# A buffer for every output block, late stores on ScalarE's queue, and two sums with x ahead of the statistics

## What is computed

```python
xn = layernorm(x)
qkv = einsum('bld,ed->ble', xn, w_qkv)          # q and k get the rotation
attn = softmax(einsum('blhd,bmhd->bhlm', q, k) * scale)
a = einsum('bld,ed->ble', einsum('bhlm,bmhd->blhd', attn, v), w_out)
f = einsum('bsh,dh->bsd', silu(xn @ wg.T) * (xn @ wu.T), wd)   # wg, wu, wd = integers / 127
out = x + a + f
```

## Time and profile before

| | us |
|---|---|
| median of 3 runs | 2934.07 (2931.21 to 2934.49) |
| the profiled execution | 2935.97 |
| its span | 2934.2 |
| PE busy | 2854.9 (97%) |
| DVE busy | 2667.8 (91%) |
| ACT busy | 2480.9 (85%) |
| POOL busy | 636.2 (22%) |

### The profile page before, as it was taken

How to read it: one execution, slowest core, us unless ns; L and a number is a source line. 1 busy time by engine, 2 the same in 40 slices (tenths; PEclk the granted TensorE clock), 3 DMA queues, 4 the chain that set the end, 5 groups by cost and what they waited for, 6 DMA issues and landing times.

```text
span 2934.2 us, 67972 instructions
## 1 busy us (share of the span) xinstructions
PE 2854.9 (97%) x27582; PEld 1052.0 (36%) x27582; DVE 2667.8 (91%) x2946; ACT 2480.9 (85%) x4639; POOL 636.2 (22%) x1214
## 2 busy tenths in 40 slices
PE   6999999999999999999999999999999999999997
PEld 4666664333333333333333333333333333333334
DVE  7667666999999999999999999999999999999952
ACT  4544555999999999999999999999999999999972
POOL 4666673011111111111111111111111111111110
PEclk9999997999999999999999999999999999999999
DMA  3233331111111111111111111111111111111125
GB/s 116 86 96 116 100 95 55 25 31 31 31 31 31 31 31 31 31 31 31 31 31 32 31 31 31 32 31 31 31 31 31 31 31 31 31 31 31 31 66 177
DMA packets 128700, 137.18 MB, mean 47 GB/s; under 512 B 43264, under 2 KB 111488, under 8 KB 128384
## 3 DMA queue, kind: packets, MB, share of 16 engines
q1 hardware_dynamic: 128384, 132.79, 16.7%
HBM read 88.15 MB, written 34.08 MB: 42 GB/s over the span
## 4 chain that ended last, share of the span: by engine, by line
PE 86%; ACT 5%; DVE 4%; issue 2%; DMA 1%; POOL 0%; SPq 0%; POOLq 0%; DVEq 0%; ACTq 0%
PE psum L764 37%; PE psum L729 21%; PE psum L800 17%; PE psum L635 5%; PE psum L606 4%; ACT probs L966 3%; ACT acc_sb L936 1%; DVE row_max L1390 1%; PE psum L650 1%; ACT hT L860 1%; DVE stats L1139 1%; PE psum L710 0%; DVE xnT L1163 0%; DVE h L1305 0%; DMA out_y<-y_in 0%
## 5 line engine op out<-in xcount | busy, mean ns | idle before, releaser
L1390 DVE TENSOR_REDUCE row_max<-psum 128x1 f32<-128x1024 f32 x2018 | 2297.2, 1217 | 23.8 <-PE psum L729 23.8
L966 ACT ACTIVATE probs<-psum 128x512 f32<-128x512 f32 x4096 | 2179.2, 595 | 159.2 <-PE psum L800 52.9
L764 PE MATMUL psum<-probs,v_op 128*32 128x256 f32 x15872 | 1297.6, 399 | 0.0
L800 PE MATMUL psum<-q_op,k_op 51*128 51x512 f16 x4096 | 854.4, 381 | 20.7 <-ACT probs L966 15.6
L729 PE MATMUL psum<-k_op,q_op 48*128 48x512 f16 x4066 | 808.0, 389 | 5.2 <-DVE row_max L1390 2.7
L729 PEld LDWEIGHTS psum<-k_op,q_op 48*128 48x128 f16 x4066 | 196.7, 93 | 853.1 <-DVE row_max L1390 543.5
L764 PEld LDWEIGHTS psum<-probs,v_op 128*32 128x32 f32 x15872 | 312.5, 108 | 525.2 <-issue 493.4
L800 PEld LDWEIGHTS psum<-q_op,k_op 51*128 51x128 f16 x4096 | 365.2, 94 | 252.3 <-ACT probs L966 70.9
L1118 POOL TENSOR_TENSOR acc_sb<-acc_sb,inv_rows 128x512 f32<-128x512 f32 x64 | 81.7, 1276 | 1682.1 <-DMA inv_rows<-inv_dram 1682.1
L635 PE MATMUL psum<-xnT,wf 128*128 128x512 f16 x768 | 179.0, 379 | 0.5 <-DVE v_space L1295 0.5
L867 ACT ACTIVATE parts<-qk_rot 128x512 f16<-128x512 f32 x64 | 40.2, 628 | 149.0 <-POOL qk_rot L1036 149.0
(11 more groups left out here) (121 smaller groups left out, 1200.6 us busy)
## 6 DMA issues: line engine op xcount, KB each, us to landing
qk_dram<-staged SPq DMA_DIRECT2D x64, 256.0 KB, 4.9
q_op<-qk_dram SPq DMA_DIRECT2D x128, 128.0 KB
k_op<-qk_dram SPq DMA_DIRECT2D x128, 128.0 KB
x_ln<-in_x SPq DMA_DIRECT2D x16, 512.0 KB, 4.4
x_res<-in_x SPq DMA_DIRECT2D x16, 512.0 KB, 5.3
y_dram<-y_blk SPq DMA_DIRECT2D x16, 512.0 KB, 3.4
k_op<-qk_dram SPq DMA_DIRECT2D x128, 64.0 KB
q_op<-qk_dram SPq DMA_DIRECT2D x128, 64.0 KB
```

Source lines behind the costliest of these rows:

```text
L764: mm = pe.matmul(bank(7)[32 * j:32 * j + 32, n0:n1], v_op[:, h % 2, t, :], probs[:, g3 % PROBS, j * BANK + n0:j * BANK + n1], start=(t == ...
L800: pe.matmul(bank(b), k_op[r:e, h % SLOTS, t * P:(t + 1) * P], q_op[r:e, h % SLOTS, j * BANK:(j + 1) * BANK], start=True, stop=True).then_i ...
L966: nc.scalar.activation(probs[:, g2 % PROBS, j * BANK:(j + 1) * BANK], bank(b), ACT.Exp, scale=to_score).then_inc(s2_used, 1)
L1390: nc.vector.tensor_reduce(row_max[:, hl % 2, t, half:half + 1], psum[:, 2 * half * BANK:(2 * half + 2) * BANK], AX.X, ALU.max).then_inc(s1 ...
```

## The change

Three things are edited. In the first stage `add_x` of tiles 0 and 1 comes ahead of `row_stats`, the other two sums behind it. At the end every output block has a buffer of its own: 8 in `y_in`, 4 in the last sequence's part of `v_space`, 4 in the first two slots of `q_op` and `k_op`; the second eight blocks are loaded on SP after `place_output(62)`, ahead of all stores, behind waits for the last `copy_v` and for the scores of heads 60 and 61. SP stores six blocks ahead of `place_output(63)`, and the other ten are stored from ACT's queue after ACT's last step. All stores share one semaphore.

```diff
--- before.py
+++ after.py
@@ -47,6 +47,8 @@
 LAG = 3
 RING = 3
 Y_BUFS = 8
+STORED_EARLY = 6
 LOWEST = -3.0e38
 DIFF_FROM = 1
@@ -226,6 +228,19 @@
             return oT_first[:, :, :, :]
         return v_space[:, (n - 1) * TILES * D:n * TILES * D].bitcast(F16).rearrange("p (a k n) -> p a k n", a=2, k=KT)
+    def y_block(k):
+        if k < Y_BUFS:
+            return y_in[:, k]
+        k -= Y_BUFS
+        if k < BLK:
+            n0 = (NT - TILES) * D + k * BLK * D
+            return v_space[:, n0:n0 + BLK * D].rearrange("p (t d) -> p t d", t=BLK)
+        k -= BLK
+        op = (q_op, k_op)[k % 2]
+        return op[:, k // 2, :].bitcast(F32).rearrange("p (t d) -> p t d", t=BLK)
     psum = keep.enter_context(nc.psum_tensor("psum", [P, 8 * BANK], F32))
     def bank(n, cols=BANK):
@@ -301,9 +316,9 @@
     o_placed = sem("o_placed")
     proj_full = sem("proj_full")
-    yin_loaded = [sem(f"yin_loaded{b}") for b in range(Y_BUFS)]
+    yin_loaded = [sem(f"yin_loaded{b}") for b in range(NBLK)]
     res_ready = sem("res_ready")
-    res_out = [sem(f"res_out{b}") for b in range(Y_BUFS)]
+    res_out = sem("res_out")
@@ -488,14 +503,13 @@
                              o_parts[32 * j:32 * j + DH, :, :]).then_inc(o_placed, 16)
         def load_y(k):
-            b, r = k % Y_BUFS, k // Y_BUFS
-            if r >= 1:
-                sp.wait_ge(res_out[b], 16 * r)
-            sp.dma_start(y_in[:, b], y_blocks[k]).then_inc(yin_loaded[b], 16)
+            sp.dma_start(y_block(k), y_blocks[k]).then_inc(yin_loaded[k], 16)
         def store_out(k):
             sp.wait_ge(res_ready, 2 * (k + 1))
-            sp.dma_start(out_blocks[k], y_in[:, k % Y_BUFS]).then_inc(res_out[k % Y_BUFS], 16)
+            sp.dma_start(out_blocks[k], y_block(k)).then_inc(res_out, 16)
         sp.wait_ge(rows_cleared, 1)
         for h in range(HEADS):
@@ -508,18 +522,15 @@
                 for k in range(Y_BUFS):
                     load_y(k)
-        STORED_EARLY = 4
+        sp.wait_ge(v_ready, HEADS)
+        sp.wait_ge(s2_used, items_before(FIRST2 + TILES * (HEADS - SLOTS + 2)))
+        for k in range(Y_BUFS, NBLK):
+            load_y(k)
         for k in range(STORED_EARLY):
             store_out(k)
-            if k >= 1:
-                load_y(k - 1 + Y_BUFS)
         place_output(HEADS - 1)
-        for k in range(STORED_EARLY, NBLK):
-            store_out(k)
-            if k - 1 + Y_BUFS < NBLK:
-                load_y(k - 1 + Y_BUFS)
-        for b in range(Y_BUFS):
-            sp.wait_ge(res_out[b], 16 * (NBLK // Y_BUFS))
+        sp.wait_ge(res_out, 16 * NBLK)
     @block.tensor
     def _(pe):
@@ -969,6 +980,10 @@
         run_steps(step)
+        for k in range(STORED_EARLY, NBLK):
+            act.wait_ge(res_ready, 2 * (k + 1))
+            act.dma_start(out_blocks[k], y_block(k)).then_inc(res_out, 16)
     @block.gpsimd
     def _(pool):
@@ -1340,9 +1355,11 @@
                 for c in range(KT):
                     x_lo(k + 1, c)
+            add_x(k, 0)
+            add_x(k, 1)
             if left >= 2:
                 row_stats(k + 2)
-            for t in range(BLK):
+            for t in range(2, BLK):
                 add_x(k, t)
             if left >= 2:
                 ln_mean(k + 2)
@@ -1358,13 +1375,12 @@
         def add_y(half):
             k, u = divmod(half, 2)
-            b = k % Y_BUFS
             if u == 0:
-                dve.wait_ge(yin_loaded[b], 16 * (k // Y_BUFS + 1))
+                dve.wait_ge(yin_loaded[k], 16)
             dve.wait_ge(proj_full, half + 1)
-            nc.vector.scalar_tensor_tensor(y_in[:, b, 2 * u:2 * u + 2, :],
-                                           bank(2 * (k % 2) + u).rearrange("p (t d) -> p t d", t=2), out_fix[:, :],
-                                           y_in[:, b, 2 * u:2 * u + 2, :], ALU.mult, ALU.add).then_inc(res_ready, 1)
+            y_half = y_block(k)[:, 2 * u:2 * u + 2, :]
+            nc.vector.scalar_tensor_tensor(y_half, bank(2 * (k % 2) + u).rearrange("p (t d) -> p t d", t=2), out_fix[:, :],
+                                           y_half, ALU.mult, ALU.add).then_inc(res_ready, 1)
         def step(c):
             hl, t = divmod(c, TILES)
```

## The result

The changed kernel takes 2928.68 us at the median of 20 runs, against 2933.16 us for the kernel before (20 runs): ratio 0.9984, 95% interval 0.9978 to 0.9991. It is 4.5 us faster, where 16.7 were forecast. The interval excludes no change at all, but the 4.5 us lie inside the 0.2% (5.9 us) that the prediction called no change, and the time is 1.2 us above its range, which ended at 2927.5.

A forecast was written before the change was run, and what follows sets the result against it. The prediction took the PE, 86% of the last-ending chain, as the bound, with savings where it stands still. First stage 9.0 plus tail 7.7 made 16.7 us off the 2934.07 median: 2917.4 us, range 2914 to 2927.5.

The forecast's parts named there:

- A: First stage, two sums ahead of the statistics: removes the PE's wait for `y_blk`, 9.0 us taken, between 0 and 9.9.
- sign of being wrong: First stage: the prediction called itself wrong if block starts stay 27.1 us apart.
- what is late next: First stage, under A: other sums and `ln_mean` up to 0.2 us later, `ln_scale` with them, PE 0.6 us earlier.
- covered, thinly: First stage, under A: with `qk_sum(2)` 0.3 us later, ACT's third `hi_part` still ends some 0.2 us before `gate(1)`.
- R2: Rival, chance 0.12: first stage gives nothing, POOL or ACT takes the place of `y_blk`; 2926.4 us.
- B: Tail, eight loads before any store: no add waits for a load; stores 0 to 2 go out at 2869.5.
- C: Tail, six stores ahead of `place_output(63)`: first sums DMA 2.1 us later, chain 2.6 us late.
- D: Tail, ten stores from ACT's queue beside `place_output(63)`: its transfers cost 0 to 3.8 us more, 2.0 taken.
- R1: Rival, chance 0.2: clock falls in the tail, four blocks cost 3 to 11 us more; 2921, at the extreme 2928.
- R3: Rival, chance 0.1: tail gives nothing, each store in turn holds up `place_output(63)`; 2927.5 us, or 2925 with half.
- R4: Rival, chance 0.04: slower, ACT's ten stores drain one after another; 2952 us, deciding from 4.6 us per store.
- R5: Rival, chance 0.04: both A and the tail fail in part; 2930 to 2934 us.

The follow-up runs named there:

- a_mean_first: Kernel before with sums 0 and 1, then statistics, then `ln_mean`, then sums 2 and 3: 2922.46 us against 2933.67, ratio 0.9964.
- a_pool_holds: a_only with GpSimd waiting for the next block's whole normalise ahead of its third low-part subtraction: 2924.14 us, ratio 0.9970 to the kernel before.
- both_hold: both, with ScalarE's ten stores waiting until head 63's o is placed: 2916.99 us, ratio 0.9947 to the kernel before.
- both_five_hold: both, with five stores on SyncE ahead of head 63's placement and ScalarE's eleven held until o is placed: 2915.47 us against 2933.46.
- both: Changed kernel with `ln_mean` directly behind the statistics, ahead of sums 2 and 3: 2918.52 us against 2934.11 for the kernel before, ratio 0.9948.
- tail_only: Changed kernel without the first-stage edit, so only the output's edit is left: 2927.70 us against 2933.67 for the kernel before, ratio 0.9981.
- a_only: Kernel before with the first-stage edit alone, two sums ahead of the statistics: 2933.37 us against 2933.67, ratio 1.0001.

## Why the prediction was wrong

**A, the first stage: 9.0 forecast, nothing came.** The prediction's own sign of being wrong came: the blocks stayed 27.14 us apart. The size of what was to be had was right. a_mean_first took 10.0 us off the time to head 0's first score, with a period of 26.41 us against the 26.4 read off block 14. The step that failed is "what is late next", which saw nothing late in POOL that could take A's gain but `qk_sum`. It followed POOL's lateness to `qk_sum` and to ACT's `gate(1)`, and found a thin cover there. It didn't follow it to POOL's own next work, the subtractions of `h_lo`, and who runs beside those. The runs showed in its place that normalise grew from 2.22 to 3.32 us under these subtractions, and that the PE waits 0.85 us per block for it, 13.4 us in all, more than the 8.1 us that went with `y_blk`. POOL is released by `ln_mean`. The change leaves it behind statistics and all four sums, as it was, but lets the PE start the next block after the first two sums alone: POOL's first `ln_scale` starts 2.3 us behind L617, where it was 1.0 behind L606, `qk_sum` 6.1 instead of 4.8 (235.81 and 235.50), and the `h_lo` rows follow into normalise. The prediction had "up to 0.2 us later" for `ln_mean` against a PE 0.6 us earlier; that makes 0.8 of the 1.3 seen. a_pool_holds, where normalise is short, has just these 0.8 (1.8 after 1.0). The other 0.5 are normalise's own work: behind the longer normalise `x_lo`, and with it sums and `ln_mean`, starts 3.0 us after the down product's start instead of 2.4 (227.49 after 224.48, 227.17 after 224.75), so the delay feeds itself. And even the 0.8 it called "covered, thinly", since it looked only for an engine that waits for POOL. The DVE didn't wait for POOL: its instructions took longer.

The row that would have warned stands in the trace of before: of the four equal `xn` instructions of a block one took 1.25 us and three 0.41. The trace thus shows that an `xn` instruction that starts under a POOL subtraction ends 0.15 us after it. One that starts first isn't held: the third of the block starts 0.17 us ahead of the subtraction of 221.77 and takes 0.41. a_pool_holds shows that all four are short when POOL's rows are kept off them but for the first 0.22 us. The Trainium skill has a rule for this ("SBUF — State Buffer", section "Who interferes with whom"): DVE and GpSimd share one pair of SBUF ports as an exclusive lock. A DVE operation in a two-port mode, which a tensor-scalar operation can take, contends for it; whichever engine issues first holds it for its whole instruction, and the other blocks. The traces agree with it, with the 0.15 us and 0.41 us above. They don't show the ports themselves, and `xn` in a form that leaves them alone wasn't tried.

**R2** (0.12, 2926.4) is what happened to the first stage: POOL took the place of `y_blk`. Its price of A, zero, was right and its way wrong, since it was argued through `qk_sum` and ACT. The evidence set against it, that block 14 ran in 26.40 us, was from a block without statistics, as the prediction itself noted, so without an `ln_mean` whose delay could be seen. It is no copy of what the edit makes, though the prediction said so.

**B held.** No add waits for a load in the tail, the eight loads went out from 2858.65 to 2866.1, the first store at 2866.18, where 2869.5 were reckoned, and nobody waited for it.

**C held.** The first sums DMA starts 1.99 us after `acc_sb` (forecast "about 2.1"), and the reciprocal comes 2.2 us later than before, where 2.6 were forecast. The PE waited 0.92 us for the DVE at half 12, with 1.3 forecast. The sums' landing behind the 0.5 MB store was hidden, as said.

**D was too low.** Between 0 and 3.8 us I took 2.0. The landings took 3.02 us (spread) and 3.30 (o), against 1.93 and 1.97 in both_hold: 2.4 us for the two. Against the kernel before, the way from the spread's first DMA to o's first grew from 7.54 us (2894.71 to 2902.25 in the earlier trace rows) to 8.99 (2894.46 to 2903.45), and from there to the PE's start from 4.01 (2906.26 in the earlier trace rows) to 5.36. That is 1.45 + 1.35 = 2.8 us for D. With C's 2.2 o came 5.0 us later, where 4.6 were forecast. The bounds for D held, the middle value was 0.8 too low. The Trainium skill ("DMA: Bandwidth & Descriptors", section "Issuing engines are not separate DMA queues") says that transfers of different issuers interleave on the same 16 DMA engines; the landings beside ACT's stores agree. What the page says of the gain, that a second issuing engine saves only issue time, no run here can show, since none has ACT's stores without the eight new buffers.

**R1 came true** (0.2 given). The PE stood still for 4.45 us, not 2.9, and the granted clock was 0.63 from 2910 to 2914. The four blocks took 12.3 us instead of the 11.2 forecast, and 10.65 at the full clock in both_five_hold, so the clock cost 1.7 us, 1.1 of it beyond the forecast. That is less than the rival's 3 to 11; in both the same matmuls took 13.12 us, a cost of 2.5.

**R3 and R4 didn't come.** The meetings on the chain of `place_output(63)` cost 2.8 us and not 12, and the last store from ACT's queue landed 3.4 us after its issue, under the 4.6 from which R4 would have decided.

**The sum.** For the tail 7.7 were forecast. Less 0.4 for o (5.0 instead of 4.6) and 1.1 for the clock, and with 0.2 for the last add and store (4.2 instead of 4.4), that makes 6.4; the profiles give 6.4, tail_only's medians 6.0. A gave nothing, and 4.5 are left of 16.7. Two misses of the same sign came together, A whole and the tail in part. The range ended at 2927.5, 1.1 us above R2 alone (2926.4), which has the tail at its full 7.7; R2 with the tail as it came is outside. R5, both in part, had 0.04 and 2930 to 2934, so the measured 2928.68 lies between the range and it.

**What stays open.** tail_only gained 6.0 us and the changed kernel 4.5; the intervals overlap, and no run tells whether the 1.5 us between them are real. The 2.8 us of the middle are in a_only's profile too, whose time is that of before, so they belong to the profiled execution of before. No run has the eight new buffers with all late stores on SP's queue, or ACT's stores with the old buffers, so how the output's 6.0 us divide between B and D isn't shown. Nor is it shown why the clock fell after 2.05 us in both_hold and not after 2.54 before the change.

## What to carry to other kernels

Moving work within an in-order engine shifts its signals against one another (here the PE was released earlier and POOL was not); follow each of them to the engine it releases, and from there to what that engine's work then overlaps, not only to who waits for it. Equal instructions with unequal durations in one block (0.41 and 1.25 us) can mark such an overlap before anything is changed. In a tail, what the last chain needs goes ahead of bulk transfers on every queue, and bulk transfers that nobody needs yet are held back until the chain is through, as long as what piles up can still drain: with eleven stores held back the pile set the end.

## What the runs showed of the hardware

- A 128x256 f32 `xn` takes 0.41 us alone and up to 1.25 when it starts under a POOL subtraction of 1.2 us, whose end it outlasts by 0.15. POOL paid little: 1.16 us alone, 1.20 to 1.26 beside the DVE.
- The granted clock fell after a PE wait of 4.45 us (the changed kernel, 0.63) and of 2.05 us (both_hold, 0.61), and not after 2.54 us before the change, 0.71 in all or 0.38 in both_five_hold. The wait's length alone doesn't decide. The next 96 matmuls took 12.32 to 13.12 us where it fell and 10.65 where it didn't.
- Small transfers on SP's queue that land in 1.9 to 2.0 us take 3.0 to 3.4 beside a stream of 0.5 MB stores that ScalarE issues.
- ScalarE needs 0.38 us to issue a 0.5 MB store in the tail of the changed kernel and 1.33 in that of both_five_hold, where the DMA engines are 85% busy.
